# Two groups' final norms held back, reset and update gates issued in two steps, and a new order of steps, in a four-layer graph kernel on one core

## The chip, the cores and the metric

One core of a Trainium2 chip runs the whole kernel. The time is the device time of one execution in microseconds (us), median of the runs shown. Engines are named as in the profile: PE is TensorE (PEld its weight loads), DVE is VectorE, ACT is ScalarE, POOL is GpSimd, SP is SyncE.

## The reference, cut to what matters

128 graphs of 128 nodes with 128 features pass four residual layers; each ends in a layer norm. The last layer is a gated recurrent unit (GRU) of five updates and is the largest part of the work.

```python
x = layernorm(x + L0(x, adj))   # graph convolutions over the first 25 nodes, in five node groups
x = layernorm(x + L1(x, adj))   # attention, 8 heads, scores + log(adj + 1e-6)
x = layernorm(x + L2(x, adj))   # normalised adjacency times (x W + b), relu
# L3: A = (adj != 0); h = x; five times:
m = h @ weight[l];  agg = A^T @ m
r = sigmoid(agg Wir + h Whr);  z = sigmoid(agg Wiz + h Whz)
n = tanh(agg Win + r * (h Whn))
h = (1 - z) * n + z * h
x = layernorm(x + h)
```

## The kernel before, in words

**Tiling.** Four graphs make a group (512 columns); groups are numbered (it, g), it from 0 to 15 and g 0 or 1. Each engine has one program: a list of steps, written out in full, that is the same in every body. A body takes about 101 us and holds two halves. In a half three threads run beside each other: A is the attention of one group, B the first layer and the third layer's front part, R the recurrent layer of two groups that take turns, slot by slot: `this` group's updates 0, 1, 2 and the `other` group's updates 3 and 4. The strings in `MERGE` say, engine by engine, from which thread the next step comes. They set the order and nothing else: what waits for what is in the steps, as semaphore waits. There are 16 + 3 bodies, since a group passes through them with a lag of up to 3; the first is done as a prologue written by hand, and the last ones hold recurrent steps only. The last group of all is called `LAST` = (15, 1). It ends alone, and its updates 3 and 4 are cut in two halves of 256 columns (`parts`).

**One update (a slot).** PE turns h into h_tok (`turn`) and multiplies it with the binary adjacency (`agg`); ACT copies the sum as agg_hi, DVE takes the rest as agg_lo; ACT copies h as h_hi, POOL takes h_lo = h - h_hi. A gate is then three products with h_hi, h_lo, h_hi and three with agg_hi, agg_hi, agg_lo, all of 512 columns (`gate`, L957): `r` six into bank RA, `hn` three into RB, `in` three into RA, `z` six into RB. ACT makes tr, un, nn and tz from them, DVE puts un and tr together (L822, L827), POOL takes hd = h - nn (L513), DVE makes the new h from hd and tz (`he` L832, `h_new` L836).

**A group's end.** `end`: PE turns h once more into RT, DVE adds x3 (y4, L843) and takes the moments (L663, L666), POOL takes the power (L458, L462). `out`: DVE makes the shift nm4 (L677), ACT scales and shifts four graphs (L527), SP stores. The same helper (L527) also makes x3 for a new group, in step `x3`, from which `begin` has PE turn it, ACT copy it twice (hT L599, h_hi L601) and POOL take h_lo.

**Fillers.** `keep_warm(n, bank)` issues n turns of the identity whose results nobody reads. Before: 16 at the start, 26 in `begin` of LAST, 38 and 8 after the update gates of LAST's updates 2 and 3 (and 8 after 4).

Of the kernel before, what the change touches and what calls it, by code (L numbers as in the profile page):

```python
# [85 lines left out]
def gated_steps(half):  # L86
# [4 lines left out]
    for n, (lag, g, layer) in enumerate(slots):  # L91
        def step(kind):
            return lag, g, kind, layer
# [3 lines left out]
        out += [step("r")]  # L97
# [4 lines left out]
        if n + 1 < len(slots):  # L102
            nxt = slots[n + 1]
            out += [(*nxt[:2], "turn", nxt[2]), step("in"), (*nxt[:2], "agg", nxt[2]), (*nxt[:2], "agg_lo", nxt[2]), step("z")]
        else:
            out += [step("in"), (*other, "end", 0), (*new, "bin", 0), (*new, "x3", 0), step("z"),
                    (*new, "begin", 0), (*other, "out", 0), step("he"), step("h_new")]
# [20 lines left out]
def gnn_stack_kernel(nc, x, adj, nodemask, W1, b1, W2, b2, fusion_w, Wq, Wk, Wv, Wo, bo, L2W, L2b,  # L128
# [3 lines left out]
    with ExitStack() as ctx:  # L132
# [32 lines left out]
        def program(eng, engine, steps, begun=()):  # L165

            for kind in begun:
                assert (0, kind) in [(lag, kind) for _, lag, g, kind, k in BODY[engine]]
            for it in range(ITERS + LAG):
                for thread, lag, g, kind, k in BODY[engine]:  # L170
                    if 0 <= it - lag < ITERS and not (it == 0 and kind in begun):
                        steps(it - lag, g, kind, k)

# [125 lines left out]

        def parts(it, g, k):  # L300
# [4 lines left out]
            return [(slice(0, W), (RT, RA, RB), 0)]  # L305

# [40 lines left out]
        def _(sp):  # L347
# [74 lines left out]
        def _(pool):  # L422
# [41 lines left out]
            def steps(it, g, kind, k):  # L464
# [41 lines left out]
                elif kind == "begin" or (kind == "turn" and k):  # L506
# [3 lines left out]
                elif kind == "z":  # L510
# [12 lines left out]
        def _(act):  # L523

            def normalise(o, y, r, n):
                for b in range(GB):
# [9 lines left out]
            def steps(it, g, kind, k):  # L536
# [58 lines left out]
                elif kind == "begin":  # L595
# [12 lines left out]
                elif kind == "agg":  # L608
                    for c, (T, _, _), d in parts(it, g, k):
                        wait_g(act, "agg_mm", g, it, k + 1 + d)  # L610
# [39 lines left out]
        def _(dve):  # L650
# [28 lines left out]
            def normalise(o, y, m, r):  # L679
                for b in range(GB):  # L680
# [533 lines left out]
```

## Time and profile before

| | us |
|---|---|
| median of 3 runs | 1719.07 (1719.02 to 1721.33) |
| profiled execution | 1718.62 |
| its span, first to last instruction | 1716.8 |
| PE busy | 1621.7 (94%) |
| DVE, ACT, POOL busy | 1366.6, 1315.0, 780.8 |
| mean granted PE clock | 0.990 of 2.4 GHz |

The profiled execution takes 1.8 us more than its span. In rows of the timeline the first number is the start in us from the span's start, the second the time from the first to the last end of the instructions in the row, then engine, line, operation, output<-inputs, shapes and count; in brackets stands how long the engine was idle before it and who ended that. PE's rows overlap: each ends later than the next begins.

### The profile page before, as it was taken

How to read it: one execution, taken by the hardware profiler on the slowest of the kernel's cores; microseconds unless marked ns; L12 is line 12 of the kernel's file. 1: busy time of each engine (PE TensorE's matmuls, PEld its weight loads, DVE VectorE, ACT ScalarE, POOL GpSimd, SP SyncE). 2: the span in 40 equal slices, each digit the busy share in tenths (PEclk: the TensorE clock that was granted, in tenths of full speed). 3: DMA queues.
4: the chain of work that ended last, by engine and by line, in shares of the span. 5: the costliest groups of instructions: out<-in, count | busy, mean ns of one | idle time of the engine just before them, and what ended most of it. 6: DMA issues, size and time to landing. Idle time of an engine off the chain costs nothing.

```text
span 1716.8 us, 34002 instructions
## 1 busy us (share of the span) xinstructions
PE 1621.7 (94%) x12192; PEld 1334.9 (78%) x12192; DVE 1366.6 (80%) x3541; ACT 1315.0 (77%) x3136; POOL 780.8 (45%) x847
## 2 busy tenths in 40 slices
PE   5689999999999999999999999999999999999996
PEld 4567787887878788787887878788787878877766
DVE  5576888878789787878979787897878888787754
ACT  2467788887878888787887887888788787877764
POOL 2233544535354453544445354453635445363432
PEclk9899999999999999999999999999999999999998
DMA  3000100001010100101001010100101000000000
GB/s 93 19 24 20 30 26 16 27 14 35 20 29 14 28 28 14 30 26 30 14 26 29 14 29 26 29 14 19 37 13 30 26 24 19 13 26 13 13 7 13
DMA packets 84801, 40.93 MB, mean 24 GB/s; under 512 B 10629, under 2 KB 84634, under 8 KB 84634
## 3 DMA queue, kind: packets, MB, share of 16 engines
q1 hardware_dynamic: 84058, 38.62, 8.2%
q8 instruction: 97, 1.59, 0.4%
q14 instruction: 70, 0.57, 0.1%
q10 hardware_dynamic: 576, 0.15, 0.0%
HBM read 30.36 MB, written 8.39 MB: 23 GB/s over the span
## 4 chain that ended last, share of the span: by engine, by line
PE 79%; DVE 11%; ACT 8%; issue 2%; POOL 1%; DMA 0%; POOLq 0%; DVEq 0%; SPq 0%; ACTq 0%
PE RA L957 17%; PE RB L957 16%; PE Q L911 8%; PE RT L1142 7%; PE RT L911 4%; PE Q L1062 4%; ACT x L527 3%; PE M L911 3%; PE Q L1077 3%; PE M L999 2%; PE M L992 2%; PE Q L1043 2%; PE M L1105 2%; DVE stats L663 2%; PE Q L1047 2%
## 5 line engine op out<-in xcount | busy, mean ns | idle before, releaser
L509 POOL TENSOR_TENSOR h_lo<-hT,h_hi 128x512 fp32r<-128x512 f32 (+1 forms) x162 | 210.6, 1301 | 545.4 <-ACT h_hi L607 516.4
L584 ACT ACTIVATE e_s<-Q,s_ng 128x128 f32<-128x128 f32 x1024 | 296.9, 401 | 19.1 <-DVE s_ng L770 17.1
L513 POOL TENSOR_TENSOR hd<-hT,nn 128x512 f32<-128x512 f32 (+1 forms) x162 | 206.3, 1274 | 32.2 <-ACT nn L623 32.1
L623 ACT ACTIVATE nn<-tr,wT 128x512 f32<-128x512 f32 (+1 forms) x162 | 117.7, 728 | 95.4 <-DVE tr L827 95.4
L615 ACT ACTIVATE tr<-RA,b_rz 128x512 f32<-128x512 f32 (+1 forms) x160 | 114.2, 714 | 98.4 <-PE RA L957 98.4
L776 DVE TENSOR_TENSOR p_s<-Q,adjTe 128x512 f32<-128x512 f32 x256 | 172.0, 683 | 20.9 <-PE Q L911 20.8
L770 DVE TENSOR_REDUCE s_ng<-Q 128x4 f32<-128x512 f32 x256 | 167.7, 681 | 9.8 <-PE Q L1062 8.5
L822 DVE SCALAR_TENSOR_TENSOR un<-tr,un 128x512 f32<-128x512 f32 (+1 forms) x162 | 109.8, 679 | 71.6 <-ACT un L619 71.6
L911 PE MATMUL Q<-ident,e_s 128*128 128x128 f32 x1024 | 155.7, 275 | 11.2 <-ACT e_s L584 11.2
L817 DVE TENSOR_TENSOR agg_lo<-RT,agg_hi 128x512 fp32r<-128x512 f32 (+1 forms) x160 | 109.4, 683 | 66.4 <-ACT agg_hi L611 64.4
L911 PEld LDWEIGHTS Q<-ident,e_s 128*128 128x128 f32 x1024 | 124.8, 141 | 35.5 <-ACT e_s L584 15.2
L458 POOL TENSOR_SCALAR ve<-mv 128x4 f32<-128x4 f32 x128 | 33.8, 264 | 246.6 <-DVE mv L666 242.3
L957 PE MATMUL RB<-h_hi,whh_hi 128*128 128x512 f32 (+1 forms) x320 | 144.0, 450 | 0.0
L957 PE MATMUL RA<-agg_hi,comp_hi 128*128 128x512 f32 (+1 forms) x320 | 139.5, 436 | 1.3
L1142 PE MATMUL RT<-a_bin,h_tok 128*128 128x128 f32 x1016 | 139.0, 280 | 1.2 <-ACT h_tok L605 0.8
L462 POOL TENSOR_TENSOR rs<-ve,half_neg 128x4 f32<-128x4 f32 x128 | 135.2, 1056 | 10.7
L627 ACT ACTIVATE tz<-RB,b_rz 128x512 f32<-128x512 f32 (+1 forms) x160 | 110.9, 693 | 36.8 <-PE RB L957 35.1
L1142 PEld LDWEIGHTS RT<-a_bin,h_tok 128*128 128x128 f32 x1016 | 124.4, 191 | 15.9 <-issue 9.6
L527 ACT ACTIVATE x<-y,nm,rs 128x128 f32<-128x128 f32 x256 | 105.1, 481 | 34.5 <-DVE nm L677 34.5
L832 DVE SCALAR_TENSOR_TENSOR hd<-tz,hd 128x512 f32<-128x512 f32 (+1 forms) x162 | 110.3, 682 | 23.8 <-ACT tz L627 21.2
L957 PE MATMUL RA<-agg_lo,comp_hi 128*128 128x512 f32 (+1 forms) x320 | 126.6, 396 | 0.4 <-DVE agg_lo L817 0.4
L957 PE MATMUL RB<-h_hi,whh_lo 128*128 128x512 f32 (+1 forms) x320 | 125.8, 393 | 0.0
(220 smaller groups left out, 4377.8 us busy)
## 6 DMA issues: line engine op xcount, KB each, us to landing
adjn<-in_adj_dram SPq DMA_DIRECT2D x32, 256.0 KB, 3.0
xin<-in_x_dram SPq DMA_DIRECT2D x32, 256.0 KB, 3.4
adjr<-in_adj_dram SPq DMA_DIRECT2D x32, 256.0 KB, 3.1
out_dram<-x SPq DMA_DIRECT2D x32, 256.0 KB, 2.4
adjc<-in_adj_dram SPq DMA_DIRECT2D x124, 4.0 KB, 2.2
xs<-in_x_dram SPq DMA_DIRECT2D x120, 16.0 KB, 1.8
W1s<-in_L_gnn_W_dram SPq DMA_DIRECT2D x1, 640.0 KB, 5.0
W2s<-in_L_gnn_W_dram SPq DMA_DIRECT2D x2, 320.0 KB, 4.9
```

Of the source, the lines that this page charges most:

```text
L462: return pool.tensor_tensor(r[:, :], v[:, :], half_neg[:, 0, 0:GB], ALU.pow)
L509: pool.tensor_tensor(h_lo[g][:, c], hT[g][:, c], h_hi[g][:, c], ALU.subtract).then_inc(SG["h_lo"][g], 1)
L513: pool.tensor_tensor(hd[g][:, c], hT[g][:, c], nn[g][:, c], ALU.subtract).then_inc(SG["hd"][g], 1)
L527: ins = act.activation(o[:, b, :], y[:, b, :], ACT.Identity, bias=n[:, b:b + 1], scale=r[:, b:b + 1])
L584: ins = act.activation(e_s[:, j, c, :], Q[j][:, c * P:(c + 1) * P], ACT.Exp, bias=s_ng[:, j, c:c + 1])
L615: act.activation(tr[g][:, c], A[:, c], ACT.Tanh, bias=b_rz[:, 0:1], scale=0.5).then_inc(SG["r_act"][g], 1)
L623: act.activation(nn[g][:, c], tr[g][:, c], ACT.Tanh, bias=bih[:, 2:3]).then_inc(SG["n_act"][g], 1)
L770: dve.tensor_reduce(s_ng[:, j, :], Q[j][:, :].rearrange("p (c k) -> p c k", c=4), AX_X, ALU.max, negate=True)\
L776: dve.tensor_tensor(p_s[:, j, :, :].rearrange("p (b h) q -> p b h q", b=2), Q[j][:, :].rearrange("p (b h q) -> p b h q", b=2, h=2), adjTe[ ...
L911: return pe.transpose(o, i, ident[0:rows, 0:rows])
L957: ins = pe.matmul(o[:, cs], weights, moving[:, cs], start=i == 0, stop=i == len(pairs) - 1)
L1142: ins = pe.matmul(T[:, q * P:(q + 1) * P], src[:, q, :], a_bin[g][:, q, :], start=True, stop=True)
```

## The change

It does nine things; the numbers of the diff's lines are those of the new file.

1. `r` becomes `r` (three products with h) and `r2` (three with agg), `z` likewise `z` and `z2`. `r2` waits for agg_hi and agg_lo before its first product; the products are the same.
2. The `MERGE` strings are new for all four engines.
3. DVE's, ACT's and POOL's `end`/`out` steps of the groups (14, 1) and (15, 0) are held back in their queues (`HELD`) until after a named step of the last groups. PE turns these two groups' h into bank Q0, which the attention no longer uses. ACT's `x3` waits for y4 of the group before in the same buffers.
4. `begin` of LAST: ACT takes h_hi from PSUM at once, DVE takes h_lo (and hT) from PSUM; `agg` of its update 0 goes to bank Q1.
5. hd of LAST's updates 2, 3, 4 is taken by DVE and no longer by POOL.
6. LAST's final scaling is shared: two graphs on ACT, two on DVE.
7. Fillers in the prologue: 56, 4, 5, 6, 20, 24 and 5 turns. In LAST: 25 and 17 in place of 38 and 8.
8. Prologue order: the first products no longer wait behind the turn of the biases, the weights are turned in 5, 6, 6 and no longer 5, 4, 4, 4, DVE's sum over adjn stands ahead of the weight copies.
9. The last two weight products (L933, L855, L856) move: PE issues them after the first score products and no longer ahead of them, and DVE copies them after the first group's second and third maximum and no longer after its `u`.

```diff
-        out += [step("r")]
+        out += [step("r"), step("r2")]
...
+        HELD = dict(
+            vector={(*NEAR_LAST[0], "end", 0): (*LAST, "x3", 0),
+                    (*NEAR_LAST[1], "end", 0): (*LAST, "h_new", LAYERS - 3), (*NEAR_LAST[1], "out", 0): (*LAST, "agg_lo", LAYERS - 2)},
+            gpsimd={(*NEAR_LAST[1], "end", 0): (*LAST, "turn", LAYERS - 2)},
+            scalar={(*NEAR_LAST[0], "out", 0): (*NEAR_LAST[1], "z", LAYERS - 2),
+                    (*NEAR_LAST[1], "out", 0): (*LAST, "z", LAYERS - 2)},
+        )
...
-                elif kind == "z":
+                elif kind == "z" and not ((it, g) == LAST and k >= LAYERS - 3):
...
+                    if (it, g) == LAST:
+                        act.activation(h_hi[g][:, :], RT[:, :], ACT.Copy).then_inc(SG["h_hi"][g], 1)
...
                 elif kind == "x3":
                     wait_g(act, "nm3", g, it, 1)
+                    if it > 0:
+                        wait_g(act, "y4", g, it - 1, 1)
...
+                    if it + g == 0 and k in (1, 2):
+                        evacuate_product(2 + k)
...
-                    if it + g == 0 and k == 1:
-                        for i in range(3, LAYERS):
-                            evacuate_product(i)
...
+                elif kind == "begin" and (it, g) == LAST:
+                    wait_g(dve, "h_hi", g, it, 1)
+                    dve.tensor_tensor(h_lo[g][:, :], RT[:, :], h_hi[g][:, :], ALU.subtract).then_inc(SG["h_lo"][g], 1)
+                    dve.tensor_copy(hT[g][:, :], RT[:, :]).then_inc(SG["h_first"][g], 1)
...
+                    if (it, g) == LAST and k >= LAYERS - 3:
+                        for c, _, d in parts(it, g, k):
+                            wait_g(dve, "n_act", g, it, k + 1 + d)
+                            dve.tensor_tensor(hd[g][:, c], hT[g][:, c], nn[g][:, c], ALU.subtract).then_inc(SG["hd"][g], 1)
...
-                        gate(A, k, 0, 0, g, "r_mm", c, d, it)
+                        gate(A, k, None, 0, g, c, True)
+                elif kind == "r2":
+                    for c, (_, A, _), d in parts(it, g, k):
+                        wait_g(pe, "agg_hi", g, it, k + 1 + d)
+                        wait_g(pe, "agg_t", g, it, k + 1 + d)
+                        gate(A, k, 0, None, g, c, False, "r_mm")
...
-                        keep_warm(38 if k == LAYERS - 3 else 8, M2)
+                        keep_warm(25 if k == LAYERS - 3 else 17, M2)
```

**PE in the prologue**, from the turns of f_t (first layer's result) to the first score products Q<-km,qT. Before:

```order
L911 MATMUL M<-ident,f_t 128x128 x4
L933 MATMUL RA<-wT 128x384
L933 MATMUL RB<-wT 128x384
L933 MATMUL RT<-wT 128x384
L911 MATMUL Q<-ident,x 128x128 x4
L1043 MATMUL Q<-xT,wT 128x512
L1044 MATMUL Q<-xT,wT 128x512
L1047 MATMUL Q<-wT,xT 128x128 x4
L933 MATMUL RA<-wT 128x384
L933 MATMUL RB<-wT 128x384
L1062 MATMUL Q<-km,qT 128x256 x8
```

Now:

```order
L956 MATMUL RB<-ident 128x128 x20
L956 MATMUL M<-ident,f_t 128x128 x4
L978 MATMUL RA<-wT 128x384
L978 MATMUL RB<-wT 128x384
L978 MATMUL RT<-wT 128x384
L956 MATMUL Q<-ident 128x128 x24
L956 MATMUL Q<-ident,x 128x128 x4
L956 MATMUL Q<-ident 128x128 x5
L1081 MATMUL Q<-xT,wT 128x512
L1082 MATMUL Q<-xT,wT 128x512
L1085 MATMUL Q<-wT,xT 128x128 x4
L1098 MATMUL Q<-km,qT 128x256 x8
```

Fillers stand ahead of and behind the turns of x, and the last two weight products have left the place ahead of the scores.

**PE at the turn of a body**, from `wo` (Q<-wT,on_ts) over the turn of x for the next attention and the first gate of the group in slot 0. Before:

```order
L1093 MATMUL Q<-wT,on_ts 128x128 x4
L911 MATMUL Q<-ident,x 128x128 x4
L1142 MATMUL RT<-a_bin,x_0 128x128 x4
L1043 MATMUL Q<-xT,wT 128x512
L1044 MATMUL Q<-xT,wT 128x512
L1047 MATMUL Q<-wT,xT 128x128 x4
L957 MATMUL RA<-h_hi,whh_hi 128x512
L957 MATMUL RA<-h_lo,whh_hi 128x512
L957 MATMUL RA<-h_hi,whh_lo 128x512
L957 MATMUL RA<-agg_hi,comp_hi 128x512
```

Now:

```order
L1131 MATMUL Q<-wT,on_ts 128x128 x4
L1184 MATMUL RT<-a_bin,x_0 128x128 x4
L956 MATMUL Q<-ident,x 128x128 x4
L994 MATMUL RA<-h_hi,whh_hi 128x512
L994 MATMUL RA<-h_lo,whh_hi 128x512
L994 MATMUL RA<-h_hi,whh_lo 128x512
L1081 MATMUL Q<-xT,wT 128x512
L1082 MATMUL Q<-xT,wT 128x512
L1085 MATMUL Q<-wT,xT 128x128 x4
L994 MATMUL RA<-agg_hi,comp_hi 128x512
```

The three h products of the gate now stand between the turn of x and the projections that need its copy xT; its agg products stay behind them.

**DVE near the end**, from LAST's update 2 (tr<-RA,un) to its update 3 (agg_lo, 128x256). Before:

```order
L827 TENSOR_TENSOR tr<-RA,un 128x512
L843 SCALAR_TENSOR_TENSOR y_0<-RT,wT,x_0 128x128 x4
L663 BN_STATS stats_0<-y_0 128x6 x4
L666 BN_AGGR mv_0<-stats_0 128x2 x4
L677 SCALAR_TENSOR_TENSOR nm_0<-mv_0,rs_0 128x4
L832 SCALAR_TENSOR_TENSOR hd<-tz,hd 128x512
L836 SCALAR_TENSOR_TENSOR hT<-hd,nn 128x512
L817 TENSOR_TENSOR agg_lo<-RT,agg_hi 128x256
```

Now:

```order
L864 TENSOR_TENSOR tr<-RA,un 128x512
L869 TENSOR_TENSOR hd<-hT,nn 128x512
L873 SCALAR_TENSOR_TENSOR hd<-tz,hd 128x512
L877 SCALAR_TENSOR_TENSOR hT<-hd,nn 128x512
L884 SCALAR_TENSOR_TENSOR y_0<-Q,wT,x_0 128x128 x4
L694 BN_STATS stats_0<-y_0 128x6 x4
L697 BN_AGGR mv_0<-stats_0 128x2 x4
L854 TENSOR_TENSOR agg_lo<-RT,agg_hi 128x256
L854 TENSOR_TENSOR agg_lo<-Q,agg_hi 128x256
L708 SCALAR_TENSOR_TENSOR nm_0<-mv_0,rs_0 128x4
```

The end of group (15, 0) has moved from ahead of the new h of LAST to behind it, and hd has come to DVE.

## Rows read from the trace of the kernel before

**Rows 1.** The page: busy time, and the granted clock in 40 slices.
```profile
PE 1621.7 (94%) x12192; PEld 1334.9 (78%) x12192; DVE 1366.6 (80%) x3541; ACT 1315.0 (77%) x3136; POOL 780.8 (45%) x847
PEclk9899999999999999999999999999999999999998
```
**Rows 2.** Windows: stretch, its length, busy time and instructions of each engine, clock, DMA.
```profile
900.00:1000.00 100.00, 97.91 (x752) 81.31 (x750) 83.38 (x218) 80.85 (x195) 47.96 (x51) 1.00 0.08 21
34.00:36.00 2.00, 1.08 (x4) 0.71 (x4) 1.97 (x6) 0.18 (x1) 0.00 (x0) 0.50 0.07 9
38.00:40.00 2.00, 2.00 (x3) 0.67 (x2) 0.00 (x0) 1.26 (x2) 0.00 (x0) 0.50 0.00 0
1690.00:1692.00 2.00, 2.00 (x11) 2.00 (x11) 0.43 (x1) 0.86 (x2) 0.02 (x1) 0.50 0.00 0
1704.00:1706.00 2.00, 2.00 (x20) 2.00 (x19) 1.30 (x4) 1.10 (x4) 0.41 (x1) 1.00 0.00 0
```
**Rows 3.** PE's waits over the span: us in total, times, longest.
```profile
PE Q L911 <- ACT o_ts L588: 14.6, 17, 1.1
PE Q L1043 <- ACT xT L572: 10.8, 16, 0.7
PE Q L1093 <- ACT on_ts L591: 6.3, 16, 0.4
```
**Rows 4.** Timeline of the prologue.
```profile
11.00 0.60 DVE L722 TENSOR_TENSOR nat<-a_c,block_p 128x424 f32<-128x424 f32 x1
12.57 0.83 PE L974 MATMUL M<-nat,sel 128*128 128x112 f32 x4
27.22 0.69 DVE L751 TENSOR_REDUCE deg<-adjn 128x4 f32<-128x512 f32 x1
34.70 1.08 PE L911 MATMUL Q<-ident,x 128*128 128x128 f32 x4 [3.43 <-DVE x L681]
36.47 2.07 PE L1043 MATMUL Q<-xT,wT 128*128 128x512 f32 x2 [0.69 <-ACT xT L572]
42.47 1.15 PE L1062 MATMUL Q<-km,qT 32*128 32x256 f32 x16
67.08 0.49 DVE L855 CAST comp_hi<-RA 128x384 fp32r<-128x384 f32 x1
69.14 0.75 DVE L790 TENSOR_TENSOR o_ns<-Q,den 128x256 f32<-128x256 f32 x2
```
**Rows 5.** Timeline at the turn of a body, and ACT's relu group of another.
```profile
1109.98 1.27 POOL L509 TENSOR_TENSOR h_lo<-hT,h_hi 128x512 fp32r<-128x512 f32 x1 [1.61 <-ACT h_hi L601]
1111.97 1.12 PE L1043 MATMUL Q<-xT,wT 128*128 128x512 f32 x2 [0.67 <-ACT xT L572]
1114.61 0.48 PE L957 MATMUL RA<-h_hi,whh_hi 128*128 128x512 f32 x1
1592.38 1.21 ACT L644 ACTIVATE a_r<-M,dinv 128x128 f32<-128x128 f32 x4
```
**Rows 6.** Timeline of LAST: end of its update 2, turn into 3, turn into 4.
```profile
1681.00 0.72 ACT L623 ACTIVATE nn<-tr,wT 128x512 f32<-128x512 f32 x1 [1.55 <-DVE tr L827]
1684.53 1.27 POOL L513 TENSOR_TENSOR hd<-hT,nn 128x512 f32<-128x512 f32 x1
1684.59 1.22 DVE L677 SCALAR_TENSOR_TENSOR nm<-mv,rs 128x4 f32<-128x4 f32 x1 [1.41 <-POOL rs L462]
1685.83 0.69 DVE L832 SCALAR_TENSOR_TENSOR hd<-tz,hd 128x512 f32<-128x512 f32 x1
1687.39 0.41 PE L911 MATMUL RT<-ident,hT 128*128 128x128 f32 x2 [1.65 <-DVE hT L836]
1695.27 1.42 POOL L513 TENSOR_TENSOR hd<-hT,nn 128x256 f32<-128x256 f32 x2 [5.25 <-ACT nn L623]
1697.69 0.44 PE L911 MATMUL RT<-ident,hT 128*128 128x128 f32 x2 [1.40 <-DVE hT L836]
```
**Rows 7.** Timeline of the last scaling.
```profile
1712.39 1.65 ACT L527 ACTIVATE x<-y,nm,rs 128x128 f32<-128x128 f32 x4 [5.76 <-DVE nm L677]
```

More of the change, by code:

```diff
@@ L103, in gated_steps @@
             nxt = slots[n + 1]
-            out += [(*nxt[:2], "turn", nxt[2]), step("in"), (*nxt[:2], "agg", nxt[2]), (*nxt[:2], "agg_lo", nxt[2]), step("z")]
+            out += [(*nxt[:2], "turn", nxt[2]), step("in"), (*nxt[:2], "agg", nxt[2]), (*nxt[:2], "agg_lo", nxt[2]), step("z"), step("z2")]
         else:
-            out += [step("in"), (*other, "end", 0), (*new, "bin", 0), (*new, "x3", 0), step("z"),
+            out += [step("in"), (*other, "end", 0), (*new, "bin", 0), (*new, "x3", 0), step("z"), step("z2"),
                     (*new, "begin", 0), (*other, "out", 0), step("he"), step("h_new")]
@@ L163, in wait_before, with program @@
                 wait(eng, name, it + g - 1, PER[name] // NG * (NG - g))
-        def program(eng, engine, steps, begun=()):
+        def program(eng, engine, steps, begun=(), first=None):
             for kind in begun:
                 assert (0, kind) in [(lag, kind) for _, lag, g, kind, k in BODY[engine]]
+            held = {}
             for it in range(ITERS + LAG):
                 for thread, lag, g, kind, k in BODY[engine]:
-                    if 0 <= it - lag < ITERS and not (it == 0 and kind in begun):
+                    if 0 <= it - lag < ITERS and not (it == 0 and kind in begun) and (it, it - lag, g, kind) != first:
+                        step = (it - lag, g, kind, k)
+                        if step in HELD.get(engine, {}):
+                            held.setdefault(HELD[engine][step], []).append(step)
+                            continue
                         steps(it - lag, g, kind, k)
+                        for late in held.pop(step, []):
+                            steps(*late)
+            assert not held, held
         ident = sb("ident", [P, P])
@@ L305, in parts, with final_parts @@
             return [(slice(0, W), (RT, RA, RB), 0)]
+        def final_parts(it, g):
+            if (it, g) in NEAR_LAST:
+                return [(slice(0, W), Q[0], 0)]
+            return [(c, banks[0], d) for c, banks, d in parts(it, g, LAYERS - 1)]
         def graphs(c):
@@ L505, in steps @@
                     root(ve[g][2], rs[g][2]).then_inc(S["ln3_pow"], 1)
-                elif kind == "begin" or (kind == "turn" and k):
+                elif (kind == "begin" and (it, g) != LAST) or (kind == "turn" and k):
                     for c, _, d in parts(it, g, k):
@@ L523, in _, with normalise @@
         def _(act):
-            def normalise(o, y, r, n):
-                for b in range(GB):
+            def normalise(o, y, r, n, graphs=GB):
+                for b in range(graphs):
                     ins = act.activation(o[:, b, :], y[:, b, :], ACT.Identity, bias=n[:, b:b + 1], scale=r[:, b:b + 1])
@@ L677, in shift, with normalise @@
                 return dve.scalar_tensor_tensor(o[:, :], m[:, :, 0], -1.0, r[:, :], ALU.mult, ALU.mult)
-            def normalise(o, y, m, r):
-                for b in range(GB):
+            def normalise(o, y, m, r, first=0):
+                for b in range(first, GB):
                     ins = dve.tensor_scalar(o[:, b, :], y[:, b, :], m[:, b, 0:1], r[:, b:b + 1], ALU.subtract, ALU.mult)
@@ L837, in steps @@
                 elif kind == "end":
[L838 removed]
+                    for n, (c, T, _) in enumerate(final_parts(it, g)):
                         wait_g(dve, "f_mm", g, it, n + 1)
@@ L1125, in steps @@
                     slot_before("agg_t", it, g, k)
-                    if k == LAYERS - 2 and it + g > 0:
+                    if k == LAYERS - 2 and it + g > 0 and (it, g) != LAST:
                         wait_g(pe, "y4", 1 - g, it + g - 1, 1)
@@ L1135, in steps @@
                     for c, (T, _, _), d in parts(it, g, k):
-                        if k == 0:
+                        if (it, g, k) == (*LAST, 0):
+                            T = Q[1]
+                            wait_g(pe, "a_bin", g, it, 1)
+                            wait(pe, "y2", it, NG)
+                        elif k == 0:
                             wait_g(pe, "a_bin", g, it, 1)
```

103 lines of the change are left out of this document (62 added, 41 removed).

## The prediction

> **What bounds the kernel now.** I read the page first. PE is busy for 94% of the span and its clock is at full nearly everywhere [rows 1]; in the middle it is busy for 97.9 of every 100 us [rows 2]. So the middle is a long queue of PE work, about fifteen bodies of 101 us, in which an edit counts only if it closes a hole between two PE instructions. The waits of PE name the holes [rows 3]: three kinds return once per body, the longest of each between 0.4 and 1.1 us. They make some 2 us per body; the sum of all products is the same before and after the change. The two ends are different. In the prologue and the first body there is one thread of work, every hand-off is exposed, and the clock falls to half: 34 to 36 us and 38 to 40 us stand at 0.50 [rows 2]. In the last 30 us only group LAST is left, again a single chain, and again 1690 to 1692 us is at 0.50: 11 products in 2 us, where 1704 to 1706 us at full clock holds 20 [rows 2]. About 100 us of ends can thus give as much as 1500 us of middle. I sum three parts, against the profiled execution's 1718.62 us.
>
> **Prologue and first body.**
> Start: PE's first products begin at 12.57, though DVE's nat was complete at 11.00 + 0.60 = 11.60 [rows 4]; the 16 fillers and the turn of the biases stood in the way. Now 56 fillers begin as soon as the identity is there, and the products come next: -0.9 us. If all 56 ran at half clock (11 records in 2 us [rows 2]) they would take 10 us and end some 1 us too late; that is the bound above, +0.1.
> DVE's sum over adjn (27.22, 0.69 long [rows 4]) stood between the last relu and the additions that wait for it; put earlier it is free: -0.6.
> From the turn of x (34.70) to the scores (42.47) it is 7.77 us now [rows 4], at half clock for most of it [rows 2]. Before that PE idles 3.43 us, which 24 fillers now cover. At full clock the turn takes half of 1.08, so the way to the projections is 36.47 - 34.70 - 0.54 = 1.23. The projections take 1114.61 - 1111.97 = 2.64 in the middle [rows 5]. Then DVE copies v, 0.69 like its sum over 512 columns [rows 4], with hand-offs 1.0. The two weight products ahead of the scores are gone. Sum 4.9: -2.9. If the clock stays low, the projections keep their length, and only the time of the two products, about 1.5, is saved.
> The last two weight products' copies took DVE from 67.08 to 69.14 [rows 4], and o_ns waited for them: -2.1. They now stand between the maxima of the first scores, ahead of ACT's exponentials. Bounds +0 (ACT's queue hides them) and +2.1 (nothing does). I take +1.4: ACT has one exponential group in hand, no more.
> Front: -5.1, bounds -8 and -1.
>
> **The middle.** At the turn of the body PE waits 0.67 us for xT [rows 5], 16 times, 10.8 us in all [rows 3]. Now r's three h products stand in that hole. They need h_lo, which POOL has at 1109.98 + 1.27 = 1111.25 [rows 5]. PE has done agg and the turn of x at 1111.97 - 0.67 = 1111.30, so r can start at once, and with its 0.7 us the projections start about 0.1 later than now: -0.55 per body. The two other holes remain: attention's weighted sum and the turn of its copy still follow each other directly in the second half, and so do `on` and `wo`, with only `begin` between.
> Against it: hn and a turn alone, 1.2 us of PE work, now stand between r2 and `in` of update 3 in the first half, where it was 3.0, and ACT has the relu group (1.21 us [rows 5]) ahead of r's tanh. Followed along ACT's queue, tanh is done about 0.3 late. In the second half a0 and the next scores have moved together with the same effect, 0.1 or so. Bounds: nothing, or a whole relu group, 1.21, per body. I take +0.35, nearer to the lower bound, since ACT is not the full engine (80.85 of 100 [rows 2]). Net -0.2 in each of 15 bodies: -3.0.
> The split itself costs nothing that I can see: the products are the same, and `r` waited for agg_hi and agg_lo after its third product before as well. ACT's new wait for y4 is met long before, except for LAST.
>
> **The tail.**
> LAST's begin: one ACT copy less, and h_lo takes 0.69 on DVE, as `he` does [rows 6], and no longer POOL's 1.27 [rows 5]. But DVE now has y4 of (14, 1), h_lo and the copy of hT ahead of agg_lo, and r2 waits for that. I put it at 0, bounds -1.8 and +1.4.
> End of update 2: nn is ready at 1681.00 + 0.72 = 1681.72. POOL, busy with the power for group (15, 0), begins hd at 1684.53; DVE stands at a shift (1684.59, 1.22 long) and makes `he` from 1685.83; PE turns at 1687.39 [rows 6]. Now DVE does hd, he, h_new in a row, 3 x 0.69 + 0.25 of hand-offs: PE turns at 1684.05. **-3.3.** The 25 fillers (2.5 us at 20 in 2 us [rows 2]) end about there. What is late next is DVE's agg_lo, behind the moments of (15, 0), which fall in while PE turns and sums; I put that at a few tenths, and r's h products cover them.
> Updates 3 and 4: from turn to turn 1697.69 - 1687.39 = 10.30. At full clock the 11 products of 1690 to 1692 take 1.1 and not 2.0 [rows 2]; the low stretch is somewhat longer than that window: -1.3. POOL's hd pair (1.42 [rows 6]) becomes two DVE steps of about 0.4: -0.35. Twice -1.65 is -3.3. If fillers don't hold the clock, twice -0.35.
> Last scaling: 1.65 on ACT for four graphs [rows 7], now two and two: -0.8.
> ACT's scaling for (14, 1) moves ahead of a tanh of LAST's update 1 in the one-after-the-other slots: bounds 0 and +1.65; as these slots are full of PE work, I take 0.
> Tail: -7.4, bounds -9 and -3.
>
> A rule that speaks against this: the shift on DVE took 1.22 us in just the time in which POOL took hd (1684.53, 1.27 long [rows 6]), on 128x4 elements. So POOL can hold DVE. DVE does more of the elementwise work in the tail now, beside POOL's h_lo; one such hold there costs up to 1.3 us, within the tail's bounds. The Trainium skill (GPSIMD Engine Reference, 8. Key points) says that GpSimd shares its SBUF interfaces with VectorE and contends with instructions of two SBUF inputs. By it each overlap of y4 or agg_lo with POOL's h_lo would lengthen LAST's chain; the trace agrees for the shift.
>
> **Sum**: -5.1 - 3.0 - 7.4 = -15.5: 1703.1 for the profiled execution. The median of the runs is 0.45 above it, so the forecast is **1703.5 us**.
>
> **The rivals.**
> A, the middle gains in full (no new hole): -0.55 x 15 = -8.3 in place of -3.0, 1698. For it: ACT and DVE have 19 and 17 us to spare in 100. Chance 0.17.
> B, fillers don't hold the clock: the tail keeps 2 x 1.3, the front gives only 2.5 of its 5.1: 1709. For it: 38 fillers ahead of 1687.39 and the clock still fell [rows 2], but 1.65 us of idleness lay between [rows 6], which the new counts close. Chance 0.13. The Trainium skill (TensorE: Matmul & The Clock Gate, What's actually happening) says that the activity monitor runs freely and doesn't begin with the kernel, so counts that fit in one run may miss in another; by it B could hold in some runs and not in others. No run here shows that yet.
> C, the held ends don't free LAST's chain, because DVE, in its queue, meets them again behind h_new: the tail gives about 4: 1707. Chance 0.09.
> D, **slower**: the new order opens a hole in each body. Mechanism: ACT stands at the relu group and one exponential group when r2 of update 3 is done, `in` waits for its tanh, and every later step of the thread is late with it. Price 1.21 + 1.1 = 2.3 per body less 0.55, 15 times: +26, less 12.5 of the ends: 1733. It decides from 12.5 / 15 = 0.8 us net per body on (1.1 for slower by over 0.2%). Against it: the same distance of 1.2 us stands in the old order at two other slots, and no wait of PE for ACT's tr is among its larger ones [rows 3]. Chance 0.07.
>
> **Numbers.** Forecast 0.54, A 0.17, B 0.13, C 0.09, D 0.07. A measurement of this kernel tells 0.2% (3.4 us) from no change. Faster by more than that: all but D and a few of B's and C's worse ends, 0.91; within: 0.04; slower: 0.05, D past its threshold. The range, 8 in 10, takes in A and most of B and C: 1697 to 1712.
>
> **What would show it.** Right: the scores' first product near 38 us; no wait of PE for xT of 0.67; waits for tr at `in` of a few tenths; the turn after LAST's update 2 about 3.3 us after nn; no 0.50 window past 1680; turn to turn 8.6 us. Wrong: PE busy below 97.9 in 100 in the middle, a half clock where the fillers stand, or a wait for DVE's h_new in LAST.

## The result, and the profile after

Median 1698.26 us in 4 runs (1697.22 to 1704.41), before 1719.05 in the runs beside it; ratio 0.9886, 95% interval 0.9859 to 0.9913. The forecast was 1703.5, the range 1697 to 1712. The profiled execution took 1697.22 us with a span of 1695.3, so the spans differ by 21.5 us. Single executions spread: 1696.44 to 1704.41 us for the changed kernel and 1713.96 to 1726.92 for the one before, over all sittings.

The page of the changed kernel, busy time and granted clock, beside [rows 1]:

```profile
PE 1628.2 (96%) x12301; PEld 1340.2 (79%) x12301; DVE 1396.5 (82%) x3550; ACT 1315.5 (78%) x3133; POOL 800.6 (47%) x841
PEclk9899999999999999999999999999999999999999
```

Windows of the changed kernel, beside [rows 2]:

```profile
900.00:1000.00 100.00, 98.34 (x753) 81.48 (x752) 85.75 (x219) 81.60 (x196) 50.44 (x51) 1.00 0.09 24
52.00:54.00 2.00, 1.14 (x5) 0.83 (x6) 1.97 (x10) 2.00 (x10) 0.00 (x0) 0.50 0.07 20
1674.00:1676.00 2.00, 2.00 (x19) 2.00 (x19) 1.26 (x4) 1.10 (x4) 0.00 (x0) 1.00 0.00 0
1682.00:1684.00 2.00, 2.00 (x19) 2.00 (x19) 0.43 (x2) 1.57 (x4) 0.00 (x0) 1.00 0.03 8
```

PE's waits over the span, beside [rows 3]:

```profile
PE Q L956 <- ACT o_ts L612: 14.0, 17, 1.1
PE Q L956 <- ACT e_s L608: 10.6, 13, 2.4
PE Q L1131 <- ACT on_ts L615: 6.7, 16, 0.7
```

The wait for xT is gone from the list, those for o_ts and on_ts stand nearly where they were, the one for e_s was there before too (11.2 us, 13 times), and no wait for tr has come. LAST's products of updates 2 to 4 now run at full clock, but the first body still has stretches at 0.50.

I took the starts of the 32 turns of x3 (PE RT<-ident,x), two per body, from both traces as marks:

| stretch | before | after | difference | forecast |
|---|---|---|---|---|
| to the second x3 turn | 149.65 | 143.21 | -6.4 | -5.1 |
| from there to the 31st | 1457.97 | 1450.37 | -7.6 | -3.0 |
| from the 31st to the end of the span | 109.2 | 101.7 | -7.5 | -7.4 |

The turn of a body in the changed kernel, timeline, beside [rows 5]:

```profile
1098.21 1.28 POOL L533 TENSOR_TENSOR h_lo<-hT,h_hi 128x512 fp32r<-128x512 f32 x1 [1.62 <-ACT h_hi L628]
1099.58 0.59 ACT L596 ACTIVATE xT<-Q 128x512 f32<-128x512 f32 x1
1099.64 0.47 PE L994 MATMUL RA<-h_hi,whh_hi 128*128 128x512 f32 x1
1100.41 1.02 PE L1081 MATMUL Q<-xT,wT 128*128 128x512 f32 x2
```

r's h products start 0.15 us after h_lo is done, and the projections follow with no wait.

LAST in the changed kernel, timeline: first its begin, where PE stands for agg_lo of update 0, then the end of update 2 and the turns into updates 3, 4 and the end, beside [rows 6]:

```profile
1637.69 0.47 PE L994 MATMUL RA<-agg_hi,comp_hi 128*128 128x512 f32 x1 [1.66 <-DVE agg_lo L850]
...
1666.55 0.72 ACT L652 ACTIVATE nn<-tr,wT 128x512 f32<-128x512 f32 x1 [1.55 <-DVE tr L864]
1666.97 2.89 PE L956 MATMUL M<-ident 128*128 128x128 f32 x25
1667.30 0.69 DVE L869 TENSOR_TENSOR hd<-hT,nn 128x512 f32<-128x512 f32 x1 [0.79 <-ACT nn L652]
1668.75 0.69 DVE L877 SCALAR_TENSOR_TENSOR hT<-hd,nn 128x512 f32<-128x512 f32 x1
1669.69 0.38 PE L956 MATMUL RT<-ident,hT 128*128 128x128 f32 x2
...
1678.45 0.44 PE L956 MATMUL RT<-ident,hT 128*128 128x128 f32 x2
...
1687.29 0.44 PE L956 MATMUL RT<-ident,hT 128*128 128x128 f32 x2
```

The last scaling, beside [rows 7]:

```profile
1691.56 0.60 DVE L712 TENSOR_SCALAR x<-y,mv,rs 128x128 f32<-128x128 f32 x2
1691.68 0.88 ACT L551 ACTIVATE x<-y,nm,rs 128x128 f32<-128x128 f32 x2 [5.31 <-DVE nm L708]
```

From the start of nn to the turn it is 3.14 us, in [rows 6] 6.39; from turn to turn 8.76 and 8.84, there 10.30.

### The profile page after: what moved, and what is told of

It is laid out like the page before. It is cut to its first block, busy times and chain, and to the rows that moved or that the text cites. A ratio compares the mean times of both kernels' runs of the same rounds, so it can differ in the third digit from the quotient of the medians.

```text
span 1695.3 us, 34409 instructions
## 1 busy us (share of the span) xinstructions
PE 1628.2 (96%) x12301; PEld 1340.2 (79%) x12301; DVE 1396.5 (82%) x3550; ACT 1315.5 (78%) x3133; POOL 800.6 (47%) x841
## 4 chain that ended last, share of the span: by engine, by line
PE 76%; DVE 10%; ACT 10%; issue 2%; POOL 1%; POOLq 0%; DVEq 0%; ACTq 0%
PE RA L994 16%; PE RB L994 15%; PE RT L1184 8%; PE Q L956 8%; PE Q L1098 4%; PE RT L956 4%; PE M L956 3%; PE M L1037 2%; PE M L1030 2%; PE Q L1115 2%; PE Q L1131 2%; DVE stats L694 2%; PE Q L1085 2%; ACT x L551 2%; PE Q L1081 2%
## 5 line engine op out<-in xcount | busy, mean ns | idle before, releaser
L533 POOL TENSOR_TENSOR h_lo<-hT,h_hi 128x512 fp32r<-128x512 f32 (+1 forms) x161 | 205.5, 1277 | 516.7 <-ACT h_hi L634 441.0
L537 POOL TENSOR_TENSOR hd<-hT,nn 128x512 f32<-128x512 f32 x157 | 202.7, 1291 | 23.6 <-ACT nn L652 23.6
L482 POOL TENSOR_SCALAR ve<-mv 128x4 f32<-128x4 f32 x128 | 45.5, 355 | 273.3 <-DVE mv L697 267.9
L486 POOL TENSOR_TENSOR rs<-ve,half_neg 128x4 f32<-128x4 f32 x128 | 159.0, 1242 | 10.7
L994 PE MATMUL RA<-agg_hi,comp_hi 128*128 128x512 f32 (+1 forms) x320 | 143.3, 448 | 4.1 <-DVE agg_lo L850 1.7
L854 DVE TENSOR_TENSOR agg_lo<-RT,agg_hi 128x512 fp32r<-128x512 f32 x159 | 109.1, 686 | 44.3 <-ACT agg_hi L640 39.5
L873 DVE SCALAR_TENSOR_TENSOR hd<-tz,hd 128x512 f32<-128x512 f32 (+1 forms) x162 | 120.3, 743 | 13.1 <-ACT tz L656 9.8
```

What stands on the lines that cost most here:

```text
L486: return pool.tensor_tensor(r[:, :], v[:, :], half_neg[:, 0, 0:GB], ALU.pow)
L533: pool.tensor_tensor(h_lo[g][:, c], hT[g][:, c], h_hi[g][:, c], ALU.subtract).then_inc(SG["h_lo"][g], 1)
L537: pool.tensor_tensor(hd[g][:, c], hT[g][:, c], nn[g][:, c], ALU.subtract).then_inc(SG["hd"][g], 1)
L873: dve.scalar_tensor_tensor(hd[g][:, c], tz[g][:, c], 1.0, hd[g][:, c], ALU.add, ALU.mult).then_inc(SG["he"][g], 1)
L994: ins = pe.matmul(o[:, cs], weights, moving[:, cs], start=start and i == 0, stop=last is not None and i == len(pairs) - 1)
```

## The experiments

The runs test the middle, the group LAST and the front; with the last of these stand the changed kernel again and two attempts at a better one. Each is the changed kernel with the edit that its text names. The period of a body is (27th x3 turn - 9th) / 9, so that an end doesn't enter; before it is 100.85 us, after the change 100.25, and 100.18 to 100.27 in the kernels that leave the bodies alone. "Theory 1" and the like point into what was expected of the run.

| kernel | median us | ratio to before, interval | period |
|---|---|---|---|
| m_old_order | 1705.62 | 0.9940 (0.9928 to 0.9953) | 100.93 |
| m_old_r_early | 1721.73 | 1.0032 (1.0016 to 1.0048) | 101.66 |
| m_r_late | 1706.75 | 0.9945 (0.9931 to 0.9959) | 100.84 |
| m_z_whole | 1705.16 | 0.9940 (0.9925 to 0.9955) | 100.70 |
| m_old_r_half0 | 1702.17 | 0.9893 (0.9874 to 0.9913) | 100.55 |
| t_hd_pool | 1702.92 | 0.9890 (0.9863 to 0.9916) | 100.18 |
| t_not_held | 1704.38 | 0.9902 (0.9874 to 0.9929) | 100.18 |
| t_38_8 | 1701.05 | 0.9885 (0.9854 to 0.9916) | 100.26 |
| f_no_24 | 1702.15 | 0.9888 (0.9862 to 0.9915) | 100.27 |
| after_again | 1698.29 | 0.9876 (0.9857 to 0.9896) | 100.21 |
| b_front | 1695.86 | 0.9859 (0.9843 to 0.9876) | 100.20 |
| b_front_a1 | 1719.68 | 0.9997 (0.9983 to 1.0010) | 101.73 |

The medians belong to three sittings, in which before took 1715.16, 1719.25 and 1718.83; the marks in the traces are finer than the ratios, and the readings rest on them. Each mark is of one execution.

### The middle

**m_old_order.** `MERGE` holds the strings of before, with a second R behind each r and z.

> The changed kernel with the order of steps of the kernel before in its bodies, and each gate's second step directly behind its first, so that r and z are six products in a row again. Prologue, held ends and fillers stay as changed. All theories: only front (-6.4 in the trace) and tail (-7.5) are left of the gain, the body is back at 100.86 us and the hole of 0.7 us at xT returns: 1705 us, ratio to the kernel before 0.992. Were it under 1702, the trace's division into three parts would be wrong, since front or tail would then give more than I read there.

Period 100.93, and the wait for xT is back. PE's waits from 400 to 1400 us:

```profile
PE Q L1081 <- ACT xT L596: 6.1, 9, 0.7
```

What the two ends give, they give without the new order; the division of the gates alone gives nothing. The median is the 1705 us that was expected; the ratio is 0.994 and not 0.992, since before took 1715.16 in this sitting.

**m_r_late.** The changed kernel with this swap on PE, in both halves:

```
-L994 MATMUL RA<-h_hi,whh_hi 128x512
-L994 MATMUL RA<-h_lo,whh_hi 128x512
-L994 MATMUL RA<-h_hi,whh_lo 128x512
 L1081 MATMUL Q<-xT,wT 128x512
 L1082 MATMUL Q<-xT,wT 128x512
 L1085 MATMUL Q<-wT,xT 128x128 x4
+L994 MATMUL RA<-h_hi,whh_hi 128x512
+L994 MATMUL RA<-h_lo,whh_hi 128x512
+L994 MATMUL RA<-h_hi,whh_lo 128x512
```

> The changed kernel with one swap in each half on PE: r's three h products of update 0 behind the projections again. Theory 1 (the hole at xT is all that the middle gains): a wait of PE for xT of 0.55 to 0.7 us returns 16 times, body 100.8 to 100.95, 1707 us (+8 to +10 against the changed kernel). Theory 2 (the new order gives part of it by itself): less than +6, 1700 to 1704 us.

PE's waits over the span:

```profile
PE Q L1081 <- ACT xT L596: 11.6, 16, 1.3
```

The period is 100.84, that of before. The swap takes back all 0.59 us per body that the middle gained: theory 1. All of it comes back in the first half of the body, 50.20 us in place of 49.60 (9th to 10th x3 turn and so on, mean of nine); the second half takes 50.64 with the swap and 50.65 without. So r's early products gain nothing in the second half. But this doesn't say that the move is enough by itself, which the next two kernels ask.

**m_old_r_early.** m_old_order, and on PE the three rows above go the other way, ahead of the projections, in both halves.

> As m_old_order (order of the bodies as in the kernel before), but on PE agg_lo and r's three h products of update 0 go ahead of the projections, in both halves; nothing else moves. Theory 1, the hole at xT is all that the middle gains: body 100.27 as in the changed kernel, 1697 to 1699 us. Theory 2, the new order closes or spares something else as well and r's early products alone give less, as h_lo or DVE is late in the old order: body 100.5 to 100.7, 1701 to 1704 us. Theory 3, r early in the old order opens another hole: 1705 us or more.

It is 0.7 us per body slower than m_old_order: theory 3. The waits of PE from 400 to 1400 us, then PE and POOL at the start of a second half:

```profile
PE RA L994 <- POOL h_lo L533: 9.4, 10, 0.9
```

```profile
1163.14 1.12 PE L1184 MATMUL RT<-a_bin,x 128*128 128x128 f32 x8
1165.20 0.47 PE L994 MATMUL RA<-h_hi,whh_hi 128*128 128x512 f32 x1 [0.94 <-POOL h_lo L533]
...
1162.54 0.19 POOL L482 TENSOR_SCALAR ve<-mv 128x4 f32<-128x4 f32 x1 [3.94 <-DVE mv L697]
1162.82 1.01 POOL L486 TENSOR_TENSOR rs<-ve,half_neg 128x4 f32<-128x4 f32 x1
1163.80 1.26 POOL L533 TENSOR_TENSOR h_lo<-hT,h_hi 128x512 fp32r<-128x512 f32 x1
```

In the second half the old order has POOL take attention's power (0.19 and 1.01 us) ahead of h_lo. In m_old_order r's products came 1.57 us after h_lo was done there and didn't notice. By halves, the first takes 49.79 us against 50.20 in m_old_order (-0.4), the second 51.87 against 50.73 (+1.1). The changed kernel has the power behind h_lo there:

```profile
1148.60 1.27 POOL L533 TENSOR_TENSOR h_lo<-hT,h_hi 128x512 fp32r<-128x512 f32 x1 [3.16 <-ACT h_hi L628]
1149.95 0.52 POOL L482 TENSOR_SCALAR ve<-mv 128x4 f32<-128x4 f32 x1
1150.55 1.46 POOL L486 TENSOR_TENSOR rs<-ve,half_neg 128x4 f32<-128x4 f32 x1
```

**m_old_r_half0.** r's products go ahead of the projections in the first half alone, where the wait for xT is.

> As m_old_order, with r's three h products of update 0 ahead of the projections in the first half alone, where the hole at xT is; the second half keeps the old order. Theory 1 (one step of PE moved in one half is what the middle gains, and m_old_r_early lost only because in the second half POOL takes attention's power ahead of h_lo): body 100.3 to 100.5 in place of 100.89, no wait for h_lo of 0.9, 6 to 9 us faster than m_old_order, ratio 0.989 to 0.991. Theory 2 (the old order as a whole can't use the early products): 100.8 or more.

Nearer to theory 1: period 100.55, just over its 100.3 to 100.5, 0.38 less than m_old_order and 0.30 more than the changed kernel. By the medians, of different sittings, it is 3.5 us faster than m_old_order and not 6 to 9. The second half (26th to 27th x3 turn, 50.70 us) is as long as in m_old_order. So the move of one step in one half gives a little over half of the gain.

Nor is the rest a hole of PE. Windows from the 9th to the 27th x3 turn, nine bodies, of before, the changed kernel and this one:

```profile
502.95:1410.58 907.63, 887.92 (x6769) 735.08 (x6769) 756.94 (x1963) 734.83 (x1756) 437.44 (x460) 1.00 0.09 24
494.74:1396.98 902.24, 886.94 (x6769) 734.78 (x6769) 774.15 (x1963) 736.16 (x1756) 453.86 (x460) 1.00 0.09 24
497.11:1402.03 904.92, 889.70 (x6769) 733.74 (x6769) 755.45 (x1963) 736.60 (x1756) 437.29 (x460) 1.00 0.09 24
```

PE is idle for 19.7, 15.3 and 15.2 us in nine bodies: this kernel has closed as much idle time as the changed one. What it lacks is in PE's busy time, 889.7 against 886.9 us for the same 6769 records. So in another order the same products take a little less or more time in sum; which of the moves does it, and why, no run here separates.

**m_z_whole.** z's agg products directly behind its h products. At the end of the first half this takes them from between `on` and `wo`:

```
 L956 MATMUL Q<-ident,o_ns 128x128 x4
-L994 MATMUL RB<-agg_hi,comp_hi 128x512
-L994 MATMUL RB<-agg_hi,comp_lo 128x512
-L994 MATMUL RB<-agg_lo,comp_hi 128x512
 L956 MATMUL RT<-ident,x_1 128x128 x4
 L1131 MATMUL Q<-wT,on_ts 128x128 x4
```

> The changed kernel with z's three agg products directly behind its three h products everywhere, so that only the reset gate is divided. My theory: the division of the update gate and where its second step stands moves no hole, 1698 us, within 2 us of the changed kernel. Rival: the second steps of z are used as filling behind attention's turns and maxima; without them a wait for e_s or o_ts grows by 0.1 to 0.3 us in each half, 1701 to 1706 us.

The rival was right in its price: period +0.45. PE's waits over the span:

```profile
PE Q L1131 <- ACT on_ts L615: 10.1, 30, 0.7
```

30 waits for on_ts where the changed kernel has 16; those for e_s and o_ts, which the rival named, did not grow. From the 9th to the 27th x3 turn PE is idle for 0.24 us more per body, which is the new wait; the other 0.21 is busy time, as in m_old_r_half0. So the second step of z is filling too, for about half of the 0.45.

### The last group

**t_not_held.**

```diff
-                    (*NEAR_LAST[1], "end", 0): (*LAST, "h_new", LAYERS - 3), (*NEAR_LAST[1], "out", 0): (*LAST, "agg_lo", LAYERS - 2)},
-            gpsimd={(*NEAR_LAST[1], "end", 0): (*LAST, "turn", LAYERS - 2)},
...
-                    (*NEAR_LAST[1], "out", 0): (*LAST, "z", LAYERS - 2)},
```

> The changed kernel, but the end and the output of group (15, 0) are no longer held back on DVE, POOL and ACT (the final turn still goes to its own bank); hd stays on DVE. Theory 1 (held ends free the chain): DVE has y4, the moments and the shift, which waits for POOL's power, ahead of hd; the turn after update 2 comes 5.0 to 5.7 us after nn's start and not 3.1, so +2 to +3 us between the turns of updates 2 and 3. Theory 2 (hd on DVE alone did it): under +0.7 us there.

Timeline of LAST's end of update 2:

```profile
1667.56 0.73 ACT L649 ACTIVATE nn<-tr,wT 128x512 f32<-128x512 f32 x1 [1.56 <-DVE tr L861]
...
1671.15 0.16 DVE L705 SCALAR_TENSOR_TENSOR nm<-mv,rs 128x4 f32<-128x4 f32 x1 [1.40 <-POOL rs L483]
1671.23 0.68 DVE L866 TENSOR_TENSOR hd<-hT,nn 128x512 f32<-128x512 f32 x1
...
1673.42 0.44 PE L953 MATMUL RT<-ident,hT 128*128 128x128 f32 x2 [2.54 <-DVE hT L874]
```

nn to turn is 5.86 us, not 3.14: +2.7, theory 1. hd on DVE is worth little while the shift for group (15, 0) is queued ahead of it. PE's idle 2.54 us were followed by a stretch at 0.50 in the trace (window 1676 to 1678, 12 products), and update 3 took 9.86 us in place of 8.76: so one such stretch goes with 1.1 us here.

**t_hd_pool.** `kind == "z"` on POOL without its exception for LAST, and hd taken out of `he` on DVE.

> The changed kernel with hd of LAST's updates 2, 3 and 4 on POOL again; the held ends stay held, so POOL has no power to take when nn comes. Theory 1 (the 3.3 us at the end of update 2 came mostly from the held ends, which leave POOL and DVE free): only 1.27 for 0.69 us at update 2 and 0.35 in each of updates 3 and 4, together +1.0 to +1.5 us in LAST's stretch. Theory 2 (hd on DVE is what gave it): +2.5 us or more at update 2 alone.

From turn to turn 11.83, 9.28 and 9.28 us, against 11.38, 8.76 and 8.84: +0.45, +0.52, +0.44, together 1.4. Theory 1. No stretch at 0.50 stands between these turns.

**t_38_8.**

```diff
-                        keep_warm(25 if k == LAYERS - 3 else 17, M2)
+                        keep_warm(38 if k == LAYERS - 3 else 8, M2)
```

> The changed kernel with 38 and 8 fillers again after the update gates of LAST's updates 2 and 3 (now 25 and 17). 38 take 1.4 us longer than 25 and stand ahead of the turn: +1.2 in every theory. Theory 1 (the counts hold the clock): 8 fillers leave PE idle for 1 us more in update 3, a window at 0.50 comes back after it, 1.3 us more, together +2.5. Theory 2 (the clock stays up because the idle stretch of 1.65 us is gone, not by the counts): no window at 0.50 ahead of the last turn, +1.2 alone.

12.82 us into update 3 (+1.44), then 8.75 and 8.85, unchanged and at full clock with 8 fillers as with 17, although 8 leave PE idle for 0.97 us ahead of the turn:

```profile
1681.61 0.44 PE L956 MATMUL RT<-ident,hT 128*128 128x128 f32 x2 [0.97 <-DVE hT L877]
```

Theory 2: the change of the counts did not end the half clock in LAST; with t_not_held, where it came back behind 2.54 us of idle time, this points at the idle time that is gone. 38 fillers only cost their length. Whether LAST needs fillers at all, no run here asks.

**The begin of LAST, in all kernels.** The hole of 1.66 us ahead of LAST's first agg products is in all thirteen kernels that have the new ends, within 0.01 us. In seven of the profiled executions (after, after_again, m_r_late, m_old_r_half0, t_not_held, b_front, b_front_a1) the clock stays up over it, and the first turn of h comes 6.2 us after the last x3 turn. In the six others (m_old_order, m_old_r_early, m_z_whole, t_hd_pool, t_38_8, f_no_24) a stretch of 3.4 us at 0.50 stands there, and it is 6.8 to 7.4 us:

```profile
1638.00:1641.00 3.00, 2.97 (x8) 2.31 (x9) 0.00 (x0) 0.72 (x2) 0.00 (x0) 0.50 0.03 5
```

This is t_38_8; the changed kernel has 16 products in the same window, at 1.00. So the tail, too, is free to vary by about 1.2 us between executions.

### The front

**f_no_24.**

```diff
-            keep_warm(24, Q[3])
             steps(0, 0, "x1_t", 0)
-            keep_warm(5, Q[3])
```

> The changed kernel without the 24 fillers ahead of the first turn of x and the 5 behind it. Theory 1 (they hold the clock for the turn, the projections and the scores): a stretch at 0.50 comes back near 33 us, the first product of the scores moves from 38.3 to 40 or 41, and +2 to +3 us are left at the end of the first body. Theory 2 (the 56 fillers at the start have raised the clock by 7 us, and it stays up over 3.5 us of idleness): no stretch at 0.50 there, the scores stay at 38.3 within 0.3.

Windows:

```profile
34.00:36.00 2.00, 1.43 (x2) 0.83 (x3) 1.93 (x5) 0.52 (x1) 0.00 (x0) 0.50 0.12 31
38.00:40.00 2.00, 2.00 (x9) 1.61 (x7) 0.00 (x0) 0.60 (x1) 1.92 (x2) 0.50 0.00 0
```

The scores start at 40.93 and not at 38.27 (+2.7), and 3.4 us are left at the second x3 turn. Theory 1.

**after_again.** No edit.

> The changed kernel once more, unchanged, as the measure for the three beside it. Ratio 0.9886 within 0.002. The last tries show that the first body comes out differently from run to run (2.4 to 23.8 us at half clock in kernels with the same prologue); I expect the stretches at 0.50 ahead of 110 us to sum to something else than the 13.6 us of the first profile, and the first x3 turn at 99.9 to shift by 0.25 to 0.3 us per us of difference.

I was wrong on the clock: 13.6 us at 0.50 again, in the same two places, and every mark of the first body within 0.15 us. But in t_hd_pool, whose prologue and first body are the same code, the stretches at 0.50 ahead of 110 us come to 23.9 us and the second x3 turn is 4.6 us later; in t_not_held to 17.1 us and 1.1 us later. So this part is free to vary by some 5 us between executions, though it need not. The Trainium skill (TensorE: Matmul & The Clock Gate, What's actually happening) has the activity monitor run freely, not started by the kernel; equal code with unequal stretches agrees with that.

**b_front.** 89 more fillers in the first body, ahead of eleven steps of attention:

```diff
+            EXTRA = {(0, "t", 3): 12, (0, "s", 1): 6, (0, "t", 4): 20, (0, "t", 7): 4, (0, "a", 1): 6, (0, "wo", 0): 5,
+                     (1, "s", 0): 6, (1, "t", 0): 11, (1, "t", 4): 7, (1, "u", 0): 5, (1, "on", 0): 7}
...
+                if it == 0 and (g, kind, k) in EXTRA:
+                    pe.wait_ge(w_comp, 3)
+                    keep_warm(EXTRA[g, kind, k], RT)
```

> The changed kernel with 89 more fillers in the first body, of 4 to 20 each, ahead of the eleven steps of attention at which PE was idle for 0.5 to 2.4 us. Theory 1 (the half-clock stretches of the first body come from these idle times): none is left ahead of 100 us, the first x3 turn moves from 99.9 to 96.5 or 97.5, and the whole is 2 to 4 us faster, 1695 us. Theory 2 (the work of that body is bound by ACT's exponentials and DVE's maxima, not by PE's clock): the clock stays up and the time moves by less than 1 us. Theory 3 (fillers stand in the way of late steps): slower by 1 us or more.

No stretch at 0.50 is left between the first 6 us and 1688 us, and the first x3 turn is at 97.59, not 99.91. The window of 52 to 54 us, which was at 0.50 in the changed kernel:

```profile
52.00:54.00 2.00, 1.55 (x13) 1.08 (x11) 1.97 (x10) 2.00 (x10) 0.00 (x0) 1.00 0.07 16
```

Theory 1, at the low end of its price: 2.3 us in the marks, 2.0 in the span against after_again (1692.7 and 1694.6). At 1695.86 it is the fastest kernel measured; its ratio's interval overlaps that of after_again, so that it beats the changed kernel is shown by the marks and not by the medians.

**b_front_a1.** b_front, and on PE (and, for its copy, on ACT) attention's second sum ahead of `in` of update 2:

```
+L1121 MATMUL Q<-p_s,vp 32x128 x16
 L994 MATMUL RA<-agg_hi,comp_hi 128x512
 L994 MATMUL RA<-agg_hi,comp_lo 128x512
 L994 MATMUL RA<-agg_lo,comp_hi 128x512
 L956 MATMUL RT<-ident,hT 128x128 x4
-L1121 MATMUL Q<-p_s,vp 32x128 x16
 L956 MATMUL Q<-ident,o_ts 128x128 x8
```

> As b_front, and the largest wait of PE in the middle, 0.8 us for o_ts once per body, is closed by order alone: in the second half attention's weighted sum goes ahead of `in` of update 2 on PE, and ACT's copy of it ahead of its tanh. Theory 1 (a hole of PE is worth its length): body 99.45 us in place of 100.27, 12 us faster than b_front. Theory 2 (in this stretch DVE is busy without a gap from y4 to the normalisation of x, and ACT nearly so, so that the hole comes back in front of `on` and `begin`): the o_ts wait goes, waits for o_ns and x3 grow by as much, body within 0.15 of 100.27.

PE's waits from 400 to 1400 us; DVE's queue in one body; windows 102 us apart:

```profile
PE Q L956 <- DVE o_ns L820: 15.3, 9, 1.7
```

```profile
999.20 1.12 DVE L884 SCALAR_TENSOR_TENSOR y<-RT,wT,x 128x128 f32<-128x128 f32 x4
1000.35 0.87 DVE L694 BATCH_NORM_STATS2 stats<-y 128x6 f32<-128x128 f32 x4
...
1001.80 0.36 DVE L816 RECIPROCAL den<-Q 128x16 f32<-128x16 f32 x2
1002.09 0.76 DVE L820 TENSOR_TENSOR o_ns<-Q,den 128x256 f32<-128x256 f32 x2
```

```profile
1004.00:1006.00 2.00, 1.60 (x9) 1.37 (x8) 1.50 (x5) 1.97 (x5) 0.39 (x2) 0.61 0.00 0
1106.00:1108.00 2.00, 1.60 (x10) 1.37 (x8) 1.55 (x5) 1.97 (x5) 0.39 (x2) 0.71 0.04 11
```

The mechanism is theory 2's, the size is not. The 0.8 us for o_ts are gone and 1.7 us for o_ns have come: den stands on DVE behind y4 and its moments. Where the clock stays up, a body takes 100.60 us (15th to 17th x3 turn), 0.4 more than in b_front. In ten bodies the longer hole is followed by 3.4 us at 0.50, and those take 101.7 to 102.2; in the others the same hole is not followed by one. By the medians this order costs 24 us.

## Why the prediction was right, and where it was not

**Front, -5.1 forecast, -6.4 measured.** The first product starts at 11.73, -0.8 (forecast -0.9). The scores start at 38.27, -4.2 in sum against -4.4: the three terms up to there hold in sum, and f_no_24 shows that the 29 fillers around the turn of x give 2.7 of it. From the scores to `on` the copies of the products were to give -0.7 and gave -0.5. The rest, -1.7 between `on` and the second x3 turn, I had no term for. In that stretch both kernels have 6.8 us at 0.50: before from 71.1 to 74.5 and from 105.2 to 108.6, where PE is busy all the time (11 products from 72 to 74 us), the changed kernel from 78.9 to 85.7, where PE is busy for 6.4 of 6.8 us. So the low stretches moved, to where a little of PE's time was idle anyway; that this gives the 1.7 us is not shown. Since equal code differs by up to 4.6 us at this mark (after_again), -6.4 and its distance from -5.1 are those of one pair of executions. The bounds of -8 and -1 had no terms behind them: those that I gave add up to -6.5 and -2.0.

**Middle, -3.0 forecast, -7.6 measured.** This is the step that failed, by a term's size: the new holes of +0.35 per body in front of `in` of update 3. The gain of -0.55 was right (0.59 when m_r_late takes it back); the loss was nothing, and the middle kept its gain in full. I had followed ACT's queue with the relu group's 1.21 us ahead of r's tanh, and set PE's distance as the only slack. No wait for tr appears in PE's list. That is rival A, to which I had given a chance of 0.17; it gave 1698 us. That it meets the measured 1698.26 so closely is luck: its middle was -8.3 and measured -7.6, its front -5.1 and measured -6.4. I was also wrong that the split costs and gives nothing beyond the xT hole: z's second step covers a wait for on_ts (m_z_whole, +0.45, of which 0.24 is idle time). And the reason that r can start at once was incomplete: I took it from the first half. In the second half the move costs 1.1 us with POOL's old order (m_old_r_early), and with the new one it gives nothing (m_r_late, 50.64 and 50.65 us). So POOL's order had to change only because the step was moved where it had no hole to fill. Last, I had said that an edit counts only if it closes a hole: of the 0.60 us per body 0.49 is idle time and 0.11 busy time of the same products.

**Tail, -7.4 forecast, -7.5 measured.** End of update 2: the turns of updates 2 and 3 lie 11.38 apart, in before 14.63, -3.25 (forecast -3.3), and t_not_held and t_hd_pool put 2.7 of it on the held ends and 0.45 on hd. Updates 3 and 4: -1.5 each (forecast -1.65); t_hd_pool gives hd 0.5 of it (forecast 0.35), which leaves 1.0 for the clock (forecast 1.3). End: from the last turn 8.0 us and not 8.8, -0.8 as forecast. The begin was 0.4 us longer and not 0: r2 waits 1.66 us for DVE's agg_lo, the mechanism that I had named and set against the copies saved. The stretch ahead of it was 1.05 shorter, of which some 0.6 would be the middle's hole once more. So the forecast terms gave -7.0 (with the begin -6.6) and the rest came from outside them; that the sum is met to 0.1 is partly luck, and so is that neither of the changed kernel's two profiled executions has the low stretch at LAST's begin. The reason that I gave for the clock there was half wrong: I named the counts with the closed idle time, and t_38_8 shows that 8 did as well as 17.

**The rule on shared ports.** DVE's shift of 128x4 took 1.22 us beside POOL's hd [rows 6] and takes 0.16 in t_not_held, where POOL has no hd beside it. That agrees with the rule of the Trainium skill (GPSIMD Engine Reference, 8. Key points) on the shared SBUF interfaces, which names DVE instructions with two SBUF inputs. But I feared it for the wrong ones: y4 and agg_lo read one of their inputs from PSUM (RT or Q). The changed kernel, update 0 of LAST:

```profile
1642.41 1.29 POOL L537 TENSOR_TENSOR hd<-hT,nn 128x512 f32<-128x512 f32 x1
1642.84 0.69 DVE L854 TENSOR_TENSOR agg_lo<-RT,agg_hi 128x512 fp32r<-128x512 f32 x1 [1.27 <-ACT agg_hi L640]
```

agg_lo takes 0.69 us with POOL beside it for its whole length, as it does without; no agg_lo of the changed kernel took longer. What the new order did bring is such a hold in the second half of each body, 14 times, where `he` now stands beside h_lo (1148.60, 1.27 long, shown above):

```profile
1148.97 1.44 DVE L873 SCALAR_TENSOR_TENSOR hd<-tz,hd 128x512 f32<-128x512 f32 x1
```

It takes 0.68 us elsewhere. PE's list has no wait from it, so it cost nothing here, but it is part of why DVE is busy for 1396.5 us and not 1366.6. None of DVE's rows of LAST shown above was held in this way. Rivals B, C and D did not occur; a new hole in each body did come in m_old_r_early and b_front_a1, but from POOL's and DVE's queue and not from ACT's.

## What to carry to other kernels

When PE is the full engine, moving a step into a hole was worth about the hole's length per body, but only where the operand's producer is early in its own queue: read that queue in every half in which the step is moved, and move it only in the half that has the hole. The longest wait in the list may be the one that hides a fuller queue behind it, so follow the chain to the next wait before closing it. In single-chain stretches look first at what is queued ahead of the chain on the elementwise engines, then at PE's idle times, which can cost a second time through the clock: in LAST those of 1.4 and 1.65 us (before) and of 2.54 us (t_not_held) were followed by a stretch at 0.50, those of 1.66 us in six executions of thirteen, and those of 0.97 us (t_38_8) were not.

## What the hardware showed that I had not expected

The same prologue and first body ran with 10.2 (t_38_8), 13.6, 17.1 and 23.9 us at 0.50 in different executions, and with none once PE's idle times were filled. In b_front_a1, with a hole of 1.7 us per body, 3.4 us at 0.50 came back in ten of the bodies in the middle, where PE is busy for 98 of 100 us in the other kernels; the first four began at 393.5, 495.9, 598.3 and 700.7 us, 102.4 us apart each time, with bodies of 101.7 to 102.2 us. The same elementwise operation of DVE takes 0.68 or 1.44 us, by whether a two-input operation of POOL runs beside it, while those that read PSUM keep their 0.69.
